# A graph network's first pass takes over four sevenths of the adjacency products of 28 destination tiles

## What is computed

```python
h = maximum(layernorm(x), 0)
Xs = h[src]
msg = where(edge_type == 0, Xs @ W_data.T + b_data, Xs @ W_control.T + b_control)
x = x + relu(segment_sum(msg, dst) + h @ W_self.T + b_self)      # first pass
h = maximum(layernorm(x), 0)
norm = rsqrt(deg)[src] * rsqrt(deg)[dst]
y, total = h, h
for _ in range(2):                                               # hop one, hop two
    y = segment_sum(y[src] * norm[:, None], dst)
    total = total + y
return x + total / 3
```

## Time and profile before

| | us |
|---|---|
| median of the three runs | 4850.95 |
| the profiled execution | 4842.59 |
| its span in the trace | 4840.8 |
| of that: sums of the first pass, first to last | 144.3 to 2641.5 |
| hop one, first sums to last | 2723.9 to 3744.4 |
| hop two, first sums to last | 3816.2 to 4833.0 |
| PE busy, share of the span | 3663.3, 76% |
| ScalarE busy | 2307.7, 48% |
| VectorE busy | 1959.6, 40% |
| POOL busy | 2869.0, 59% |

### The profile page before, as it was taken

How to read it: one execution, slowest core, us unless ns; L and a number is a source line. 1 busy time by engine, 2 the same in 40 slices (tenths; PEclk the granted TensorE clock), 3 DMA queues, 4 the chain that set the end, 5 groups by cost and what they waited for, 6 DMA issues and landing times. The chain is left out here.

```text
span 4840.8 us, 59773 instructions
## 1 busy us (share of the span) xinstructions
PE 3663.3 (76%) x22243; PEld 3001.0 (62%) x22243; DVE 1959.6 (40%) x3213; ACT 2307.7 (48%) x3075; POOL 2869.0 (59%) x3055
## 2 busy tenths in 40 slices
PE   7345766677667767666767699898897789998898
PEld 4334444444444444434444688888887688888888
DVE  7213666666666667667666011111112111111111
ACT  4001433333333434334334566666666566666666
POOL 2666665666665666666664556655663565655654
PEclk9555555555555555555556799999998899999999
DMA  5222332323232323233233455555555455555554
GB/s 186 58 53 67 95 92 87 107 90 91 91 107 91 91 91 105 92 95 107 92 103 97 123 149 153 154 156 150 154 151 168 130 148 139 145 144 146 145 144 132
DMA packets 367258, 571.63 MB, mean 118 GB/s; under 512 B 66678, under 2 KB 308225, under 8 KB 359283
## 3 DMA queue, kind: packets, MB, share of 16 engines
q1 hardware_dynamic: 270435, 370.74, 24.4%
q0 software_dynamic: 95664, 196.60, 16.1%
q10 hardware_dynamic: 864, 0.39, 0.0%
HBM read 424.48 MB, written 142.99 MB: 117 GB/s over the span
## 5 line engine op out<-in xcount | busy, mean ns | idle before, releaser
L863 POOL DMA_INDIRECT rows<-typed_table,index x1661 | 1584.4, 954 | 953.6 <-issue 503.1
L863 POOL DMA_INDIRECT rows<-hop_table,index x1306 | 1246.4, 954 | 943.3 <-PE sums_bank L1079 471.2
L999 ACT CAST strip_ring<-stage 128x1792 fp32r<-128x1792 uint8 x840 | 1376.3, 1685 | 751.4 <-remote 384.2
L1188 PE MATMUL wide<-table_parts,strip_ring 128*128 128x256 f32 x11760 | 1567.2, 296 | 112.4 <-issue 60.2
L1188 PEld LDWEIGHTS wide<-table_parts,strip_ring 128*128 128x128 f32 x11760 | 1525.7, 204 | 130.6 <-issue 108.3
L990 ACT CAST stage<-wide 128x392 uint8<-128x392 f32 x1920 | 801.3, 502 | 1356.1 <-PE wide L1150 878.4
L1079 PE MATMUL sums_bank<-hot,rows 128*128 128x80 f32 x5934 | 1095.1, 347 | 291.4 <-issue 240.9
L1150 PE MATMUL wide<-stage 128*128 128x392 bf16 x1920 | 755.1, 490 | 671.6 <-ACT stage L990 309.8
L1079 PEld LDWEIGHTS sums_bank<-hot,rows 128*128 128x128 f32 x5934 | 1047.1, 263 | 328.7 <-issue 325.5
L1150 PEld LDWEIGHTS wide<-stage 128*128 128x128 bf16 x1920 | 185.6, 110 | 1196.7 <-ACT stage L990 525.2
L1550 DVE TENSOR_TENSOR stage<-count_up,stage 128x1568 bf16<-128x1568 f32 x480 | 851.3, 1773 | 0.0
(11 more groups left out here) (140 smaller groups left out, 936.4 us busy)
## 6 DMA issues: line engine op xcount, KB each, us to landing
stage<-strips SPq DMA_DIRECT2D x840, 224.0 KB
strips<-stage SPq DMA_DIRECT2D x60, 1568.0 KB
rows<-typed_table,index POOLq DMA_INDIRECT x1661
rows<-hop_table,index POOLq DMA_INDIRECT x1306
hop_table<-scaled SPq DMA_DIRECT2D x50, 256.0 KB
resid<-xin SPq DMA_DIRECT2D x50, 256.0 KB
xin<-resid SPq DMA_DIRECT2D x50, 256.0 KB
typed_table<-rows SPq DMA_DIRECT2D x49, 256.0 KB, 2.1
```

Of the source, the lines that this page charges most:

```text
L863: pool.indirect_dma_start(out=rows[:, o % RING, c, :], out_offset=None, in_=tables[k], in_offset=bass.IndirectOffsetOnAxis(ap=index[:, chu ...
L999: act.copy(strip_ring[:, number % STRIP_RING], counts_ring[place]).then_inc(strip_cast, 1)
L1188: last = pe.matmul(wide[:, nth % 4, 0:PARTS * P], strip_ring[:, number % STRIP_RING, b - first, :], table_parts[:, b, :, :].rearrange("p n ...
```

## The change

- Hop one takes 16 batches (64 tiles) from the matrix, hop two still 15. So the matrix has 64 tiles and 512 quads (34 slots with 2, and 148 with 3), still in slots 24 to 205; hop one's gathers begin at group 135, it has 73 slots instead of 82.
- Of the 28 tiles of batches 1, 3, 5, 7, 9, 11 and 13 the first four pieces (112 steps) are made in the first pass, from slot 124 on, over 72 slots: 56 slots have two such steps, 16 none. Each has a load by SP (`load_early`), a cast by ScalarE (`cast_early`) into a ring of two strips, and 14 matmuls by TensorE (`early_step`); every four there is a `read_early` on VectorE, and every 16 a store of 256 KB by SP.
- Hop one keeps 64 x 7 - 112 = 336 steps, 318 of them over 71 slots. For the 28 tiles, SP loads the kept sums back, and `read_tile` adds them with two additions instead of one reduction.
- The early steps need a PSUM bank: it is taken from the cells, CELL_BANKS goes from 3 to 2.
- The two strips and three rings of counts lie where the table's parts of blocks 56 to 75 are to stand. These 20 blocks are not split when their batches end but are loaded back and split in four turns in slots 200 to 203 (`load_held`, `part_held`).

The core of the diff:

```diff
-CELL_BANKS = 3
-DENSE_BATCHES = 15
+CELL_BANKS = 2
+EARLY_BANK = 2
+SMALL_BANK = 3
+HOP_BATCHES = (0, 16, 15)
+DENSE_BATCHES = max(HOP_BATCHES)
-DENSE_SLOTS = 80
+LAST_FREE = 2
+EARLY_BATCHES = (1, 3, 5, 7, 9, 11, 13)
+EARLY_PIECES = 4
+EARLY_START = 124
+EARLY_SLOTS = 72
+EARLY_RING = 2
+EARLY_COUNTS = 3
+HELD_BLOCKS = 5
+HELD_START = 200
...
+    early_slot = [EARLY_START + j // EARLY_PIECES * EARLY_SLOTS * EARLY_PIECES // len(early_steps) + j % EARLY_PIECES * 2 // EARLY_PIECES
+                  for j in range(len(early_steps))]
...
+                def load_early(j):
+                    tile, piece = early_steps[j]
+                    if j == 0:
+                        sp.wait_ge(fresh_made, early_first // NODE_BLOCKS)
+                    if j >= EARLY_COUNTS:
+                        sp.wait_ge(early_cast, j - EARLY_COUNTS + 1)
+                    sp.wait_ge(strips_stored[tile % 2], 16 * (tile // 2 + 1))
+                    sp.dma_start(early_counts[j % EARLY_COUNTS], strips[tile][:, piece * STEP_BLOCKS:(piece + 1) * STEP_BLOCKS, :]
+                                 ).then_inc(early_in[j % EARLY_COUNTS], 16)
...
+                def cast_early(j):
+                    act.wait_ge(early_in[j % EARLY_COUNTS], 16 * (j // EARLY_COUNTS + 1))
+                    if j >= EARLY_RING:
+                        act.wait_ge(early_used, j - EARLY_RING + 1)
+                    act.copy(early_strips[:, j % EARLY_RING], early_counts[j % EARLY_COUNTS]).then_inc(early_cast, 1)
...
-                            for quad in quads_of_slot(i):
+                            early = early_at(i)
+                            if held_at(i - 1) is not None:
+                                part_held(held_at(i - 1))
+                            for n, quad in enumerate(quads_of_slot(i)):
+                                for j in early[n:n + 1]:
+                                    cast_early(j)
                                 for w in range(QUAD):
                                     keep_cell(quad * QUAD + w)
...
+                def early_step(j):
+                    tile, piece = early_steps[j]
+                    nth, first = j // EARLY_PIECES, piece * STEP_BLOCKS
+                    if j == 0:
+                        pe.wait_ge(low_ready, parts_before(early_first))
+                    if piece == 0 and nth:
+                        pe.wait_ge(early_read, nth)
+                    pe.wait_ge(early_cast, j + 1)
+                    for b in range(STEP_BLOCKS):
+                        last = pe.matmul(wide[:, EARLY_BANK, 0:PARTS * P], early_strips[:, j % EARLY_RING, b, :],
+                                         table_parts[:, first + b, :, :].rearrange("p n f -> p (n f)"),
+                                         start=(piece == 0 and b == 0), stop=(piece == EARLY_PIECES - 1 and b == STEP_BLOCKS - 1))
+                    last.then_inc(early_used, 1)
...
-                            for quad in quads_of_slot(i):
+                            early = early_at(i)
+                            for n, quad in enumerate(quads_of_slot(i)):
                                 make_cells(quad)
-                        elif k and i < hop_groups:
+                                for j in early[n:n + 1]:
+                                    early_step(j)
...
+                    if k == 1 and q in EARLY_BATCHES:
+                        dve.wait_ge(early_back, 16 * (EARLY_BATCHES.index(q) + 1))
+                        dve.tensor_tensor(into, wide[:, nth % 4, 0:P], into, ALU.add).then_inc(half_read, 1)
+                        dve.wait_ge(half_read, EARLY_BATCHES.index(q) * NODE_BLOCKS + b + 1)
+                        dve.tensor_tensor(into, wide[:, nth % 4, P:PARTS * P], into, ALU.add).then_inc(tile_read, 1)
+                        return
...
+                def read_early(n):
+                    m, b = divmod(n, NODE_BLOCKS)
+                    if b == 0 and m >= 2:
+                        dve.wait_ge(early_stored[m % 2], 16 * (m // 2))
+                    dve.wait_ge(early_used, (n + 1) * EARLY_PIECES)
+                    dve.tensor_reduce(own_in[:, m % 2, b * P:(b + 1) * P],
+                                      wide[:, EARLY_BANK, 0:PARTS * P].rearrange("p (n f) -> p f n", n=PARTS), AX_X, ALU.add
+                                      ).then_inc(early_read, 1)
```

More of the change, by code:

```diff
@@ L609, in gnn_kernel @@
         assert all(lead_steps[k] <= LEAD_AT_ONCE * LAST for k in range(1, HOPS + 1))
+        last_early = {tile: slot for (tile, _), slot in zip(early_steps, early_slot)}
+        assert all(slot_of_quad((tile + 1) * QUADS - 1) + 3 <= early_slot[j] for j, (tile, _) in enumerate(early_steps))
+        assert event_slot(early_first // NODE_BLOCKS - 1) + 4 <= EARLY_START - 1 and early_slot[-1] + 4 <= HELD_START
+        assert 22 == max(s for s in range(total) if event_slot(s) + 3 < HELD_START) and event_slot(23) + 3 > HELD_START + len(held)
         def edge_round(i):
```

215 lines of the change are left out of this document (152 added, 63 removed).

## The result

The changed kernel takes 4938.2 us (median of four runs, 4935.9 to 4939.7) against 4850.0 for the kernel before (four runs on the same chip, 4839.1 to 4865.0). The ratio is 1.018, with a 95% interval of 1.016 to 1.021: the change makes the kernel slower, by about 88 us (whether by more than 2% the interval leaves open). The prediction was 4975, with a range of 4785 to 5120 and 0.66 on slower. The profiled execution took 4937.6 us, its span is 4935.8; the span before was 4840.8, so 95.0 us were added.

What follows compares the result with a forecast made beforehand. TensorE was taken to bound the hops, its handshake with ScalarE and VectorE's quads the first pass. Terms: -185 + 64 + 90 + 150 + 5 = +124 us on 4842.6, so 4967, as median 4975; range 4785 to 5120.

Steps and rivals of the forecast that it cites:

- Hop one: Hop one: 84 steps and nine slots fewer, TensorE still the bound; 185 us gained, bounds 113 to 192.
- the new slot of 11.6 us: Hop one: 4.48 steps a slot at 1.85 us, plus 3.30 for sums and rest, instead of 12.60.
- rival 4: Hop one's slot stays at 12.60 us; gain 113 instead of 185, kernel 5047 us; chance 0.12.
- Quads: First pass: 32 more quads at 2.46 us, half price inside the early stage; 64 us lost, bounds 0 to 79.
- Two banks: First pass outside the early stage: cells at 0.54 us instead of 0.40 in bursts; 90 us lost, bounds 0 to 121.
- Early steps: Slots 124 to 195: 112 steps at 2.5 us, 280 in all, less 130 of cover; 150 us lost.
- The cover of 130 us: Slots 124 to 195: PE's idle time before cells takes 130 of the early steps' 280 us.
- rival 1: Slots 124 to 195: dense early steps raise TensorE's clock, the stage gives -24 us, kernel 4750; chance 0.18.
- What else moves: Casts, reads, loads, stores, held blocks and TensorE's new waits: 5 us lost, range 0 to 30.
- Rival 2: Slots 124 to 195: 206 us of idle time cover early steps, leaving 74; kernel 4822 us; chance 0.12.
- Rival 3: First pass: early steps crawl beside gathers at 25 us each; five such add 110, kernel 5085 us; chance 0.10.

Runs made afterwards that it cites:

- e1: Two PSUM banks for cells instead of three, in the kernel before: 5087.6 us against 4999.8, ratio 1.0168.
- e2: Changed kernel with hop one back at 15 batches (480 quads) and early steps for six batches, 96 instead of 112: 5110.0 us.
- e10: Kernel before with two PSUM banks for cells instead of three, and without hop two's gathers: 4732.3 us against 4846.9.
- e3: Changed kernel with early steps for five batches instead of seven, 80 instead of 112: 5086.3 us, ratio 1.0167 to the kernel before.
- e4: Changed kernel with early steps cut from 14 matmuls to 2, loads, casts, waits and reads kept: 4906.2 us; kernel before 4999.8.
- e7: Changed kernel with three banks for cells again, `count_up` moved from PSUM to SBUF as int16: 4785.1 us against 4005.9 for the kernel before, ratio 1.1945.
- e9: Kernel before with only `count_up` moved from PSUM to SBUF, as int16: 4907.5 us, ratio 1.2241.
- e6: Kernel before with hop two's steps cut from 14 matmuls to 11, gathers kept: hop two 809.1 us, 22 less.
- e8: Kernel before without the gathers of the first pass's groups 60 to 203 and of all hop two: 3881.4 us.

## Why the prediction was right, and where it was wrong

The direction and the size (+124 predicted, +95 measured in the span) were right, and of the mechanisms that of the banks. The size owes much to luck: three stages are off by 85, 22 and 41 us and offset each other, and the largest loss, the early steps, came out at its size by another way than the one forecast. Point by point:

- **Hop one, -185 predicted, -144 measured: mis-sized.** The nine slots that go are worth 9 x 12.60 = 113 us. The step that failed is the new slot of 11.6 us: the slot measured 12.17, so 0.43 shorter instead of 1.0. The prediction priced a removed step by its busy time (1.85) in a slot where PE was busy 89% and took the rest, 0.94 a slot, as turns and waits that would stay. It had the other end in its bounds, 113 for unchanged slots, and the truth lies somewhat nearer to that end. In the trace of after, slots with 4 steps take 12.12 us, with PE idle for 1.98, and slots with 5 take 12.53, idle 1.35: the slots differ by 0.4 us. Over the whole hop the price of a step was higher, 0.43 / 0.55 = 0.8 us on chip A and 0.9 from e1 to e2, and still half of 1.85; the other pairs on chip B scatter around that. These are averages with the slots at the end: the first 66 slots average 12.01 us, and 12.58 before. Why a step is worth so little is not shown; e10 has a hold-up of 2.3 us a group that goes with gathers and not with steps, and that fits.

The steps of hop one in the kernel before (2774 to 3730 us) and the groups of the changed kernel (2970 to 3820 us), counterparts of the earlier trace rows over nearly the whole hop:

```profile
L1188 PE MATMUL wide<-table_parts,strip_ring 128*128 128x256 f32 x5264 | 696.4, 295 | 26.1 <-ACT strip_ring L999 14.2 <-issue 11.1
...
L1338 PE MATMUL wide<-table_parts,strip_ring 128*128 128x256 f32 x4332 | 600.2, 299 | 64.3 <-issue 45.3 <-ACT strip_ring L1114 18.1
...
L978 POOL DMA_INDIRECT rows<-hop_table,index x543 | 521.7, 961 | 302.3 <-issue 145.5 <-PE sums_bank L1211 91.1 <-remote 65.7
```

PE's idle time before steps is 64.3 us where it was 26.1, the growth being nearly all "issue", that is without a cause that the profile shows. Before the sums it fell at the same time, 78.3 us by "issue" before and 47.3 after. Steps and sums together have 89 us of it in 956 and 93 in 850, 1.2 and 1.3 us a slot: it moved from the sums to the steps and did not shrink with them. That a group of steps had 9 us of idle time before was read as a sign that TensorE is the bound and that rival 4 is unlikely; it said only that steps were not what waited; the idle time lay before the sums, 70.8 us in the same group of rows, 69.9 of it by "issue".

- **Quads, +64 predicted, about +10: over-sized.** The price of 2.46 us came from two neighbouring slots. The pair is not odd: the means of slots 24 to 123 differ by 2.39. But the same chip with 480 and with 512 quads differs by 0.3 to 0.5 us a quad (e2 against e3 and e4), from which the 10 is an estimate for all 32. The difference between the slots of one trace was not the price of a quad more. That a late quad makes the next slot easier would explain it and was not tested.

- **Two banks, +90 predicted, +84 to +100 measured: right in sum.** The burst (4.3 us predicted, 4.25 seen), the round of 1.08 us and the total hold. From a quad's first copy to its fourth it went from 1.14 to 1.47 us in the median, 0.33 more, in every trace with two banks. That makes 0.33 x 2.6 quads = 0.87 a slot, of which 0.55 was paid (e10). The banks were the prediction's mechanism, and they are shown by themselves on chip B (+84) and, by stages, on chip E; how the sum divides among the stages is known to some 35 us only, the gap between e1 and e2. The lower clock in these slots (0.55 to 0.50) was not foreseen. And 44 of the 100 us fell in the stage where the prediction had none.

- **Early steps, +150 predicted, +143 measured: right in size, by another way.** Slots 124 to 195 grew by 187 us; 44 are the banks' (e10). Of the remaining 143 nearly all go with the matmuls (e4). Steps took 281.6 / 112 = 2.51 us in the mean (2.5 predicted), the clock was 0.72 (below 0.8 predicted). The cover of 130 us has its size, 281.6 - 143 = 139, but it is not what the prediction took it for, idle time of PE. PE's idle time in the stage is 902.0 - 641.8 = 260 us with two banks and no steps (e10; 263 in e1) and 1046.0 - 783.8 = 262 with them: the steps took none of it. What gave way is PE's other work. Without the early steps it is busy for 783.8 - 281.6 = 502 us, where e10 has 642, although it makes 48 cells more. Under the higher clock (0.72 against 0.50) the records of the sums fell from 255.6 to 213.2 us and those of the cells from 332.3 to 297.1; the rest of the 140 is records that overlap, and the ends of records are modelled. So the faster clock, rival 1's mechanism, paid for over half of the cover and idle time for nothing, and that it came to the size of the idle time that the prediction had counted is luck.

- **What else moves, +5 predicted.** The stages not named above add up to 2 us, and all that comes with an early step except its matmuls costs 6 (e4).

- **Rival 1** (the clock rises) came halfway: 0.72 in the stage and 0.75 while steps run, short of the 0.89 at which it would have decided. On chip C, where TensorE isn't held up, the stage has 0.87 and grows by 75 us, banks and quads included; that it loses all the same is due to slots 24 to 123. The rule of the Trainium skill, TensorE: Matmul & The Clock Gate, Part 1, that stood beside this rival is half borne out: the dense steps did lift the clock, from 0.56 to 0.72 on chip A and from 0.67 to 0.87 on chip C, but not to the top. **Rival 2** (idle time takes the steps) is refuted on chip A by the idle time before cells, 265.3 and 262.2 us; it is what happens where POOL binds (e7 against e9). **Rival 3** (crawl beside gathers) did not occur: the 112 early steps took 1.90 to 3.45 us. **Rival 4** (hop one's slot stays) is over half true: of 1.0 us of shortening 0.43 came.

- **The errors in the stages** offset each other in part: slots 24 to 123 came 85 us under their terms, slots 124 to 195 22 over, and hop one gave 41 less. The hit of +124 against +95 owes much to that. The single errors add up to 148 us, and the sum is off by 29.

Open: why gathers in flight hold TensorE up on some chips and not on others, and by what path; whether they do so in the first pass; why a quad more costs so little; the split of the 114 us on chip C between bank and quads; the 35 us of e1; and early steps with three banks and `count_up` left in PSUM, which was not tried. None of the kernels that do the whole work came in under the kernel before.

## What to carry to other kernels

Don't price work that is added or removed by its busy time, nor by the difference between slots of one trace: here a step of 1.85 us busy was worth 0.8 us of a slot on chip A, where slots with five and with four steps differ by 0.4, and a quad cost some 0.4 us where the slots differ by 2.4. A kernel with only that count changed gives the price. For a PSUM bank taken from a handshake between two engines, divide the round (here 1.08 us) by the banks and compare it with the slower engine's own time (0.40): that could be worked out from two rows, and the burst of eight copies came out at 4.25 us where 4.3 was predicted. Check where a cover comes from, too: a sum can come out right while the idle time that it counted on stays as it was. And look for a floor in each engine before moving work: the same edit cost the same 95 us on two kinds of chip by wholly different stages. On one of them POOL's 8 x 1.25 us is the floor of the stages before the change (e6, e8), and on the other TensorE, held up beside gathers, is above that.

## What the runs showed of the hardware that was not expected

- One and the same kernel takes 4003 to 4006 us on two chips and 4847 to 5000 on three. In the hops the difference is TensorE beside indirect gathers: hop two without gathers is 831.0 us on chip E and 831.3 on chip C; with them it is 1016.8 on chip A and 831.3 on chip C, and hop one on chip E is 1023.7.
- Beside VectorE instructions with both inputs in SBUF (one of them the row as int16), POOL's gather instruction takes 1490 ns in the mean; with the row in PSUM (fp32) it takes 957. VectorE's own instructions differ by 5 ns. It made the kernel 22% slower (e9).
- With two banks for the cells the granted clock of slots 24 to 123 is 0.50 on chips A, B, C and E, where it was 0.55 (A) and 0.65 (C) with three; with early steps the stage behind has 0.72 (A) and 0.87 (C). On chip A PE is busy there for 502 us beside its early steps; with two banks and no steps it is 642 (E) and 641 (B).
